# Image attention by GpSimd and by the output projection, idle products at the start, another order of exponentials

## The chip, the cores and the metric

The kernel runs on one core of a Trainium2 chip. The metric is the device time of one execution in microseconds, from start to end on that core.

## What is computed

Two cross-attention layers follow each other over a batch of 8, each on x of 256 rows by 320 channels, 20 heads of 16. The second has an image part with four image tokens; its weights are a softmax over the sum of scaled scores and a semantic term. Cut to what matters:

```python
# layer 0: text tokens 0..76, image tokens 77..255 of the context, two softmaxes
q, k, v = heads(x @ Wq.T), heads(text @ Wk.T), heads(text @ Wv.T)
out = softmax(q k^T / 4) v + softmax(q k_ip^T / 4) v_ip
x = out @ Wo.T + bo + x
# layer 1: text tokens 0..251, four image tokens
probs_t = softmax(q k^T / 4)
qsem = l2norm(probs_t @ text)                    # per head, 512 channels
sem = qsem @ l2norm(ip).T                        # per head, 4 tokens
probs_ip = softmax(q k_ip^T / 4 + 0.5 * sem) * mask[s]
out = probs_t v + probs_ip v_ip
x = out @ W_out + b_out + x
```

## The kernel before

A unit u is one batch element of one layer: units 0 to 7 are layer 0, 8 to 15 layer 1. A unit has ten steps (NP), one for each pair of heads; q = 10u + j counts steps. `plan(u, j)` (L96) writes out by hand the order of the work of a step, and every engine's program walks through the same plan and issues what is its own, in that order. A stretch u = -1 of ten steps stands ahead of unit 0. All waits are on counting semaphores.

What a step has, as TensorE sees it:

- `scores(q+1)` (L468, products at L476): two chunks of 512 columns for the next pair of heads. ScalarE makes exponentials of them into P (`weights`, L795). In layer 1 it first makes rounded ones into PH (`rounded_weights`, L786), chunk 0 and 1, and then the plain ones, chunk 0 and 1.
- in layer 1, GpSimd subtracts PH from P (Y, L1221), TensorE multiplies PH by the context's Gram matrix (`quad`, L480, products at L490), and VectorE multiplies both (Y, L1002); this gives the norm of qsem.
- `weigh` (L494) in every even step: values, the Gram part and the sums of four heads into the bank pPV (L508 and L512, in layer 1 L517 and L522; L522 waits for VectorE's Y of the last head pair). ScalarE takes it out (`evacuate`, L805, into Vs), `values_back` (L526, L531) transposes it, VectorE's `normalize` (L1004) divides and stores O and ST. GpSimd's `norms` (L1228) takes the power -0.5.
- `maximum(u+1, h)` (L447, L453): the row maxima of the next unit's scores, reduced by VectorE (L984, L985, L987, L989) into m_sb; how many fall into a step is in MAXH and, for u = -1, MAXF. `shift_rows` (L464) transposes them; rows go by DMA into the operand QP (L695, the high ones on ScalarE's queue in layer 0, the low ones on SyncE's), and `scores` of that unit wait for them.
- pieces of `prepare(u+2)` (L392, L374): the projections of the unit after next, so many products in each step as PACE says, and FIRST for u = -1. A job that ends has "done" in the plan; SyncE then stores its result (`store_queries`, `store_keys`) and later loads it as head rows (`load_queries`, `load_keys`, L671 and L679); the maxima wait for these.

The image part of a unit u of layer 1 is done in unit u+1: `image_softmax` (L1035, with the sum, the exponential by ScalarE at L827) in step 1, `image_shares` (L1054, w4 at L1068) in step 2, then one product per image token, w4 by the value row VB (`image_product`, L706, into one of two tiles TI that lie in VX), by GpSimd, and one addition to O for each by VectorE (`image_add`, L1081), in steps 3 to 5. For unit 14 VectorE does the products as well; the last unit is cut into heads 0 to 11 and 12 to 19, part of the first being done inside the unit. Then `attention_back` (L535, L545) transposes O in step 6, ScalarE and VectorE split it into ahi and alo (L714, L906), and `output` (L550, L560) multiplies by wo in steps 7 and 8, VectorE adds the residual (L1104), SyncE stores. At the very end `last_output` (L564, L572) runs in two parts, each behind its transposes. In layer 0 the same is in steps 1, 2, 4 and 5 of the next unit. `image_tokens` (L576, L583 to L595) makes the image keys, values and norms once, in step 3 of unit 1.

TensorE takes banks from a pool of seven, the one given back longest ago, and waits then until its last reader is done (`freed`, `take`). A DMA and a wait of SyncE hold up all that stands behind them on its queue. The values VB of the next image part are loaded on SyncE in step 5 (L1331).

## Time and profile before

| what | value |
|---|---|
| runs, us | 840.23, 841.76, 843.2 (median 841.76) |
| the profiled execution, us | 841.76 |
| its span, first to last instruction, us | 840.0 |
| mean granted clock of TensorE | 0.965 of 2.4 GHz |
| busy, share of the span | TensorE 92%, VectorE 71%, ScalarE 50%, GpSimd 45% |
| DMA | 101.94 MB, mean 121 GB/s |

Names of engines in the rows: PE is TensorE's products, PEld its weight loads, DVE VectorE, ACT ScalarE, POOL GpSimd, SPq and ACTq the queues that issue DMAs. A line such as L453 is one of the code. "x2" are two instructions that follow each other, and the time is from the start of the first to the end of the last; products overlap, since their drain is counted in. In brackets stands how long the engine stood idle before, and what ended it. The granted clock is given as a share of 2.4 GHz: 0.5 is the lower level, 1.2 GHz.

### The profile page before, as it was taken

The numbers are of one execution on the slowest core, as the hardware profiler recorded it, in microseconds if no ns is written. First come the engines' busy times: TensorE is split into PE (matmuls) and PEld (weight loads), VectorE is DVE, ScalarE is ACT, GpSimd is POOL, SyncE is SP. The second block draws the span as 40 slices with busy tenths as digits, with TensorE's granted clock in tenths as the row PEclk, the third lists the DMA queues.
The fourth block names the chain that finished last, engine by engine and source line by source line (L and its number), as shares of the span: only waits on it lengthen the run. The fifth ranks groups of instructions, "written<-read, shape, count | busy, mean of one in ns | idle before, by whom it ended". The sixth has DMA issues, their size and how long they took to land.

```text
span 840.0 us, 17139 instructions
## 1 busy us (share of the span) xinstructions
PE 773.8 (92%) x6304; PEld 626.1 (75%) x6304; DVE 594.3 (71%) x1571; ACT 424.1 (50%) x907; POOL 379.6 (45%) x283
## 2 busy tenths in 40 slices
PE   5679899999999999999999999999999999887774
PEld 5678688888888877877877777878777777654452
DVE  4357355757577576858679689698796895976784
ACT  5234535464636565565455564654655645444420
POOL 6421112020202031225587577676865776758561
PEclk9799999999999999999999999999999999999795
DMA  8865734665637463744263173351541533110010
GB/s 257 224 181 150 185 107 120 200 161 152 171 101 217 118 197 90 205 106 139 67 159 114 47 183 98 78 169 52 134 131 44 142 98 80 30 47 20 30 34 16
DMA packets 103171, 101.94 MB, mean 121 GB/s; under 512 B 10152, under 2 KB 102064, under 8 KB 103088
## 3 DMA queue, kind: packets, MB, share of 16 engines
q1 hardware_dynamic: 101552, 99.54, 42.7%
q10 hardware_dynamic: 1536, 1.31, 0.5%
q8 instruction: 50, 0.82, 0.4%
q14 instruction: 33, 0.27, 0.1%
HBM read 62.93 MB, written 36.74 MB: 119 GB/s over the span
## 4 chain that ended last, share of the span: by engine, by line
PE 68%; DVE 16%; issue 6%; DMA 4%; ACT 3%; POOL 1%; SPq 1%; ACTq 0%; DVEq 0%; POOLq 0%
PE pB L374 20%; PE pB L490 11%; PE pB L453 7%; PE pB L476 7%; PE pB L560 5%; DVE m_sb L987 4%; PE pPV L512 4%; PE pPV L522 4%; PE pPV L517 3%; PE pB L531 3%; PE pPV L508 2%; DVE Y L1002 2%; DVE O L1081 2%; DMA KP<-k0d 1%; PE pB L545 1%
## 5 line engine op out<-in xcount | busy, mean ns | idle before, releaser
L1221 POOL TENSOR_TENSOR Y<-P,wv 128x512 f32<-128x512 f32 x120 | 157.2, 1325 | 146.2 <-ACT P L803 146.1
L1002 DVE TENSOR_TENSOR Y<-pB,Y 128x512 f32<-128x512 f32 x160 | 107.9, 683 | 58.1 <-PE pB L490 49.9
L453 PE MATMUL pB<-KP,QP 96*128 96x256 f32 x640 | 131.0, 289 | 11.9 <-DMA KP<-k0d 10.3
L453 PEld LDWEIGHTS pB<-KP,QP 96*128 96x128 f32 x640 | 108.3, 193 | 24.8 <-DMA KP<-k0d 6.8
L476 PE MATMUL pB<-QP,KP 100*128 100x512 f32 x320 | 111.8, 427 | 9.8 <-DMA QP<-mhi 4.5
L987 DVE TENSOR_REDUCE m_sb<-pB 128x2 f32<-128x504 f32 x160 | 107.6, 674 | 9.6 <-PE pB L453 8.7
L1198 POOL TENSOR_TENSOR klo<-xin,khi 128x256 fp32r<-128x256 f32 x18 | 13.2, 756 | 217.2 <-ACT khi L714 217.2
L803 ACT ACTIVATE P<-pB 128x512 f32<-128x512 f32 x160 | 86.5, 596 | 43.5 <-PE pB L476 33.7
L803 ACT ACTIVATE P<-pB,ln 128x512 f32<-128x512 f32 x160 | 101.3, 693 | 0.0
L793 ACT ACTIVATE wv<-pB 128x512 fp32r<-128x512 f32 x120 | 66.9, 592 | 65.1 <-PE pB L476 64.8
L714 ACT ACTIVATE Vs<-pPV 128x512 f32<-128x512 f32 (+1 forms) x80 | 39.4, 493 | 118.9 <-PE pPV L512 72.5
L984 DVE TENSOR_REDUCE m_sb<-pB 128x2 f32<-128x154 f32 x160 | 49.8, 311 | 49.3 <-PE pB L453 48.8
L985 DVE TENSOR_REDUCE m_sb<-pB 128x2 f32<-128x358 f32 x160 | 83.2, 520 | 0.0
L490 PE MATMUL pB<-wv,wk 128*128 128x512 f32 x250 | 77.9, 416 | 0.1
L374 PE MATMUL pB<-chi,wki 128*128 128x180 f32 (+3 forms) x384 | 71.3, 274 | 0.0
L374 PE MATMUL pB<-khi,wq 128*128 128x256 f32 (+1 forms) x288 | 58.5, 300 | 8.4 <-DVE wq L906 8.4
L476 PEld LDWEIGHTS pB<-QP,KP 100*128 100x128 f32 x320 | 51.4, 193 | 16.5 <-DVE Y L1002 5.8
L1228 POOL TENSOR_TENSOR rn<-n,mhalf 128x8 f32<-128x8 f32 (+2 forms) x17 | 57.8, 3397 | 12.2 <-DVE n L1033 12.1
L374 PE MATMUL pB<-wvi,chi 128*128 128x320 f32 x256 | 62.1, 312 | 0.2 <-POOL wvi L1211 0.2
L374 PEld LDWEIGHTS pB<-chi,wki 128*128 128x128 f32 (+1 forms) x384 | 56.1, 172 | 6.0 <-issue 4.1
L490 PEld LDWEIGHTS pB<-wv,wk 128*128 128x128 f32 x250 | 45.2, 194 | 18.6 <-issue 10.7
L522 PE MATMUL pPV<-Y,y 128*32 128x256 f32 x640 | 44.5, 398 | 12.4 <-DVE Y L1002 12.4
(159 smaller groups left out, 1698.2 us busy)
## 6 DMA issues: line engine op xcount, KB each, us to landing
QP<-q0d SPq DMA_DIRECT2D x64, 192.0 KB, 4.0
KP<-k0d SPq DMA_DIRECT2D x64, 192.0 KB, 4.2
c_sb<-in_cT SPq DMA_DIRECT2D x16, 512.0 KB, 4.9
q0d<-qhi SPq DMA_DIRECT2D x32, 256.0 KB, 2.5
k0d<-khi SPq DMA_DIRECT2D x30, 256.0 KB, 2.5
VB<-vipd SPq DMA_DIRECT2D x8, 640.0 KB, 3.6
q0d<-qlo SPq DMA_DIRECT2D x16, 256.0 KB, 2.7
k0d<-klo SPq DMA_DIRECT2D x15, 256.0 KB, 2.6
```

The lines of the kernel that those rows point to most:

```text
L374: made = mm(out, l, r, start=(n == 0), stop=(n == len(pairs) - 1))
L453: made = mm(bank[:, sc * S:sc * S + S], QP[i][0:KROWS, j, a, sc * 128:sc * 128 + 128], KP[i][0:KROWS, j, :], start=True, stop=True)
L476: mm(bank[:, :], KP[i][0:QROWS, j, ch * 128:ch * 128 + 128], QP[i][0:QROWS, j, :, :].rearrange("p a s -> p (a s)"), start=True, stop=True) ...
L490: made = mm(bank[:, :], G[i][:, col:col + 128], ph[src], start=(n == 0), stop=(n == len(jobs) - 1))
L522: made = mm(pPV[32 * j:32 * j + 32, 0:S], y21[:, :], Y[:, p, ch, ss], start=False, stop=(ch == 1), tile_position=(0, 32 * j))
L793: act(PH[q % HR][ch], bank_of["sc", q, ch][:, :], ACT.Exp, scale=0.25).then_inc(ac_ph, 1)
L803: act(P[:, q % PR, ch, :], bank_of["sc", q, ch][:, :], ACT.Exp, scale=0.25, **twice).then_inc(ac_exp, 1)
L985: nc.vector.tensor_reduce(m_sb[:, :, H + h], v[:, :, TXT0:S], AX, ALU.max).then_inc(dv_mx, 1)
L987: nc.vector.tensor_reduce(m_sb[:, :, h], v[:, :, 0:TXT1], AX, ALU.max)
L1002: tt(Y[:, p, dst, :], bank_of["gp", q, dst][:, :], Y[:, p, dst, :], MUL).then_inc(dv_y, 1)
L1221: tt(Y[:, p, ch, :], P[:, p, ch, :], PH[q % HR][ch].bitcast(F32), SUB).then_inc(po_y, 1)
L1228: tt(rn[:, :, hs], n2[:, :, hs], mhalf[:, 0:2 * n].rearrange("p (c h) -> p c h", c=2), POW).then_inc(po_rn, 1)
```

## The change

What it does, part by part:

1. **Start.** After `prepare(0)` TensorE issues thirty products of 512 columns whose result nobody reads (`repeat`). FIRST is 9 products in each of the steps 0 to 8 of u = -1 and 30 in step 9 (before 12 in eight steps, 8 and 7). In steps (0, 0) and (1, 0) the first maximum stands behind the weigh part and two of the three pieces, no longer ahead of them.
2. **Exponentials.** ScalarE's order in layer 1 is rounded 0, plain 0, rounded 1, plain 1; in even steps the evacuation stands behind rounded 0.
3. **Image part of units 8 to 13** ("folded"): GpSimd makes four products and the three additions of them in TI (`image_step`, one step of seven at the end of step 2, two at the end of steps 3, 4 and 5); VectorE adds once, in step 6. The transposes are in step 7, the output in 8 and 9. VB is loaded in step 7. w4 has a tile of its own.
4. **Image part of units 14 and 15** ("closing"): the image values of the heads are laid out as block-diagonal tiles bdh and bdl (`image_values`, VectorE, six products with a mask hmask that a new DMA loads, and two memsets once), multiplied by wo to Mb (nine products of TensorE, taken out by ScalarE); w4 is transposed (two, `image_weights_back`, wT by ScalarE); Mb and wT are one more product, in f32, in each chunk of the output. O of these units holds the text part alone. For unit 14 this is in steps 2 to 6 of unit 15; for unit 15 bd and Mb are in steps 7 and 8, and all else behind the last values: transposes of O, the 24 products of the output, the image softmax, shares, transposes, copy and three products.
5. **image_tokens** also makes the values transposed (twelve more products), split into vhi and vlo. cip, csq, vhi, vlo and the mask share a tile.

The diff, cut:

```diff
-FIRST = (12, 12, 12, 12, 12, 12, 12, 12, 8, 7)
+FIRST = (9, 9, 9, 9, 9, 9, 9, 9, 9, 30)
+LATE_MAX = ((0, 0), (1, 0))
...
+    elif (u, j) in LATE_MAX:
+        out += scores + weigh
+        rest = heads
...
+    if u > B and folded(u - 1):
         if j == 1:
-            out += [("soft", u - 1, 0)]
+            out += [("soft", u - 1)]
         if j == 2:
-            out += [("shares", u - 1, 0), ("mix", u - 1, 0, 0)]
+            out += [("shares", u - 1)]
+        out += [("mix", u - 1, n) for n in {2: (0,), 3: (1, 2), 4: (3, 4), 5: (5, 6)}.get(j, ())]
+        if j == 6:
+            out += [("add", u - 1)]
+        if j == 7:
+            out += [("ot", u - 1, 0), ("ot", u - 1, 1)]
+        if j in (8, 9):
+            out += [("op", u - 1, (8, 9).index(j))]
+    elif u > B:
+        if j == 1:
+            out += [("soft", u - 1)]
+        if j == 2:
+            out += [("shares", u - 1), ("ot", u - 1, 0)]
         if j == 3:
-            out += [("mix", u - 1, 0, 1), ("mix", u - 1, 0, 2), ("add", u - 1, 0, 0)]
+            out += [("ot", u - 1, 1), ("wt", u - 1), ("bd", u - 1)]
         if j == 4:
-            out += [("mix", u - 1, 0, 3), ("add", u - 1, 0, 1), ("add", u - 1, 0, 2)]
-        if j == 5:
-            out += [("add", u - 1, 0, 3)]
-        if j == 6:
-            out += [("ot", u - 1, 0), ("ot", u - 1, 1)]
-        if j in (7, 8):
-            out += [("op", u - 1, j - 7)]
+            out += [("mb", u - 1)]
+        if j in (5, 6):
+            out += [("op", u - 1, j - 5)]
...
+    if (u, j) == (U - 1, 7):
+        out += [("bd", u)]
+    if (u, j) == (U - 1, 8):
+        out += [("mb", u)]
...
+                if u == U - 2:
+                    pe.wait_ge(ac_wt, closing_no(u))
+                    pe.wait_ge(ac_mb, closing_no(u))
...
+                    if u == U - 2:
+                        made = mm(bank[0:M, n * S:n * S + S], Mb[:, m * 128:m * 128 + M], wT[:, :], start=False, stop=True)
...
+            def last_image(u):
+                pe.wait_ge(ac_wt, closing_no(u))
+                pe.wait_ge(ac_mb, closing_no(u))
+                for m in range(KC):
+                    mm(bank_of["op", u, m][0:CHUNK[m], 0:S], Mb[:, m * 128:m * 128 + CHUNK[m]], wT[:, :],
+                       start=False, stop=True).then_inc(pe_op, 1)
...
+                bank = take("idle", n)
+                for _ in range(n):
+                    mm(bank[:, :], wki[:, 0, 0, 0:128], wki[:, 0, 1:3, 0:256], start=True, stop=True)
+                give(bank)
...
             for _ in prepare(0):
                 pass
+            repeat(30)
...
                 for ch in range(2):
+                    if ch and q >= B * NP:
+                        rounded_weights(q, ch)
...
+                for v, dst in ((vhi, bdh), (vlo, bdl)):
+                    for k in range(KC):
+                        K = CHUNK[k]
+                        made = tt(dst[0:K, k], v[0:K, k, None, NIP * b:NIP * b + NIP].bitcast(F32).to_broadcast([K, H, NIP]),
+                                  hmask[0:K, k, :, None].to_broadcast([K, H, NIP]), MUL)
+                made.then_inc(dv_bd, 1)
...
+                if n in (0, 1, 3, 5):
+                    tt(heads(TI[:, at]), w4[:, :, :, token:token + 1].to_broadcast([128, 2, H, D]),
+                       heads(VB[:, token, None, :].to_broadcast([128, 2, C])), MUL).then_inc(po_q, 1)
+                else:
+                    tt(TI[:, 0], TI[:, 0], TI[:, 1], ADD).then_inc(po_mix if n == 6 else po_q, 1)
...
-                    if u >= B and j == 5:
+                    if folded(u) and j == 7:
                         load_image_values(u)
```

## Rows read from the trace of the kernel before

**Rows 1.** Busy time by stretch: us, engines' busy time, granted clock, DMA, GB/s.

```profile
32.70:59.10 26.40, 21.84 (x154) 21.53 (x154) 17.14 (x49) 6.43 (x18) 2.09 (x3) 0.88 0.69 190
...
93.40:142.00 48.60, 44.82 (x387) 36.83 (x385) 25.14 (x76) 20.77 (x49) 9.63 (x7) 0.96 0.49 136
142.00:179.70 37.70, 37.62 (x347) 31.79 (x344) 24.67 (x74) 20.24 (x46) 4.26 (x6) 1.00 0.66 181
...
537.60:593.50 55.90, 55.15 (x443) 44.35 (x442) 46.32 (x117) 31.27 (x66) 38.27 (x26) 1.00 0.40 111
...
705.30:758.20 52.90, 46.22 (x341) 33.09 (x340) 40.82 (x100) 25.85 (x50) 37.76 (x26) 0.94 0.22 57
758.20:805.00 46.80, 37.03 (x242) 24.82 (x241) 33.24 (x59) 22.35 (x43) 32.13 (x20) 0.85 0.07 23
805.00:840.00 35.00, 18.31 (x122) 11.79 (x120) 22.16 (x53) 4.25 (x11) 12.62 (x11) 0.71 0.09 28
```

**Rows 2.** Timeline, TensorE, before unit 0: start, us, engine line, shapes, [idle before].

```profile
32.72 0.80 PE L453 MATMUL pB<-KP,QP 96*128 96x256 f32 x2 [6.56 <-DMA KP<-k0d]
...
59.10 1.85 PE L476 MATMUL pB<-QP,KP 100*128 100x512 f32 x4 [4.54 <-DMA QP<-mhi]
```

**Rows 3.** Timeline, TensorE, from the start of unit 1.

```profile
99.22 0.47 PE L453 MATMUL pB<-KP,QP 96*128 96x256 f32 x2 [3.78 <-DMA KP<-k0d]
...
100.08 1.68 PE L512 MATMUL pPV<-P,VY 128*32 128x256 f32 x16
...
109.91 1.05 PE L512 MATMUL pPV<-P,VY 128*32 128x256 f32 x16
...
116.37 2.45 PE L583 MATMUL pB<-cip,Y 128*128 128x32 f32 x24
118.75 2.34 PE L589 MATMUL pB<-Y,cip 128*32 128x320 f32 x8
```

**Rows 4.** Timeline, GpSimd, steps 2 to 6 of unit 11.

```profile
560.61 1.34 POOL L706 TENSOR_TENSOR VX<-tw,VB 128x640 f32<-128x640 f32 x1 [0.74 <-DVE tw L1068]
...
578.30 1.30 POOL L1221 TENSOR_TENSOR Y<-P,wv 128x512 f32<-128x512 f32 x1 [2.42 <-ACT P L803]
```

**Rows 5.** Groups by shape, GpSimd: the full two-input pass of 640 elements.

```profile
L1208 POOL TENSOR_TENSOR wo<-c_sb,wo 128x640 fp32r<-128x640 f32 x1 | 1.6, 1553 | 3.0 <-ACT wo L714 3.0
```

**Rows 6.** Instructions on the tile VX (TI): minimum, median and maximum in ns.

```profile
L1081 DVE TENSOR_TENSOR O<-O,VX x36: 424/817/2030, 452.7 to 830.1; 128x640 f32<-128x640 f32 x28, 128x384 f32<-128x384 f32 x4, 128x256 f32<-128x256 f32 x4
L706 POOL TENSOR_TENSOR VX<-tw,VB x28: 643/1337/1925, 448.9 to 829.0; 128x640 f32<-128x640 f32 x24, 128x384 f32<-128x384 f32 x2, 128x256 f32<-128x256 f32 x2
```

**Rows 7.** Timeline, unit 14, steps 4 to 6.

```profile
737.08 3.13 DVE L1081 TENSOR_TENSOR O<-O,VX 128x640 f32<-128x640 f32 x2
...
742.13 1.93 PE L522 MATMUL pPV<-Y,y 128*32 128x256 f32 x16 [2.92 <-DVE Y L1002]
```

**Rows 8.** Timeline, unit 15, steps 4 to 6.

```profile
784.48 1.89 PE L490 MATMUL pB<-wv,wk 128*128 128x512 f32 x7
...
794.63 1.93 PE L522 MATMUL pPV<-Y,y 128*32 128x256 f32 x16 [4.51 <-DVE Y L1002]
```

**Rows 9.** Timeline, the end of unit 15 and of the kernel.

```profile
805.78 0.25 DVE L1043 TENSOR_TENSOR t<-ST,invip 128x96 f32<-128x96 f32 x1
...
806.06 1.22 DVE L1046 TENSOR_TENSOR t<-t,rn 128x96 f32<-128x96 f32 x1
...
817.74 1.93 PE L522 MATMUL pPV<-Y,y 128*32 128x256 f32 x16 [3.03 <-DVE Y L1002]
...
820.90 0.21 DVE L1015 RECIPROCAL rs<-pB 128x8 f32<-128x8 f32 x1 [2.16 <-PE pB L531]
...
822.03 1.89 POOL L1228 TENSOR_TENSOR rn<-n,mhalf 128x8 f32<-128x8 f32 x1 [2.34 <-DVE n L1033]
...
834.01 1.05 PE L572 MATMUL pB<-ahi,wo 128*128 128x256 f32 x4
...
837.02 0.47 DVE L1113 SCALAR_TENSOR_TENSOR xres<-pB,bo,xres 64x256 f32<-64x256 f32 x1 [0.58 <-PE pB L572]
```

More of the change, by code:

```diff
@@ L63, in norms_no, with folded, closing_no @@
     return 2 * (u - B) + list(norm_parts(u)).index(g) + 1
[L66 to L89 removed]
+def folded(u):
+    return B <= u < U - 2
+def closing_no(u):
+    return u - (U - 2) + 1
 def thirds(n):
@@ L344, in freed @@
                     pe.wait_ge(dv_y, 2 * (a - B * NP) + what[2] + 1)
+                elif kind == "idle":
+                    pass
                 elif kind == "nt":
@@ new lines, in image_values @@
+            def image_values(u):
+                bank = take("mb", u)
+                pe.wait_ge(dv_bd, closing_no(u))
+                pe.wait_ge(lo_w["o1"], 1)
+                pairs = []
+                for k in range(KC):
+                    h_, l_ = (v[:, k].rearrange("p h n -> p (h n)") for v in (bdh, bdl))
+                    pairs += [(h_, wo[:, 0, k, :]), (h_, wo[:, 1, k, :]), (l_, wo[:, 0, k, :])]
+                for _ in chain(bank[0:H * NIP, 0:C], pairs, pe_mb):
+                    pass
+                give(bank)
@@ new lines, in image_tokens @@
+            def image_tokens():
+                for i, w in enumerate((wki1, wvi1)):
+                    bank = take("ip", i)
+                    pe.wait_ge(l_w["ip1"], 32)
+                    pe.wait_ge(l_w["const"], 16 * 6)
+                    for m in range(KC):
+                        M = CHUNK[m]
+                        for k in range(EC):
+                            made = mm(bank[0:M, 32 * m:32 * m + 32], w[:, k, m * 128:m * 128 + M], cip[:, k, :],
+                                      start=(k == 0), stop=(k == EC - 1))
+                    made.then_inc(pe_ip, 1)
+                    give(bank)
@@ L597, in image_tokens, with repeat @@
                 give(bank)
+                bank = take("ip", 3)
+                for k in range(EC):
+                    made = mm(bank[0:B * NIP, 0:C], cip[:, k, :], wvi1[:, k, :], start=(k == 0), stop=(k == EC - 1))
+                made.then_inc(pe_ip, 1)
+                give(bank)
+            def repeat(n):
+                bank = take("idle", n)
+                for _ in range(n):
+                    mm(bank[:, :], wki[:, 0, 0, 0:128], wki[:, 0, 1:3, 0:256], start=True, stop=True)
+                give(bank)
             for _ in prepare(0):
                 pass
+            repeat(30)
             for u in range(-1, U):
@@ L633, in tensor_program @@
                 attention_back(U - 1, part)
[L634 removed]
+            last_output(U - 1)
+            image_weights_back(U - 1)
+            last_image(U - 1)
         def two(bank, M, n):
@@ L891, in scalar_program @@
             evacuate(U - 1, NG - 1)
-            image_weights(U - 1, 1)
-            attention_back(U - 1, 0)
-            attention_back(U - 1, 1)
+            for part in range(2):
+                attention_back(U - 1, part)
+            image_weights(U - 1)
+            image_weights_back(U - 1)
         def low_c(u):
```

326 lines of the change are left out of this document (159 added, 167 removed).

## The prediction

> **What bounds the kernel now.** I read the windows by unit first. The page has no single limit: in layer 1 TensorE is full, at both ends it is not. Unit 11 stands for units 10 to 13: TensorE is busy 55.15 of 55.90 us, VectorE 46.32, GpSimd 38.27, so nothing done beside TensorE there is worth more than 0.75 us [rows 1]. The start is different: in the stretch before the first scores TensorE is busy 21.84 of 26.40 us at clock 0.88, and unit 1 takes 48.60 us where unit 2 takes 37.70 [rows 1]. The end is worst: in unit 14 TensorE is busy 46.22 of 52.90 us, then 37.03 of 46.80 at clock 0.85, then 18.31 of 35.00 at 0.71 [rows 1]. So each part of the change is priced in its own stretch. The profiled execution took 841.76 us, which is also the median of the three runs; the span is 840.0, so 1.76 lies around it and the sum is made from 841.76.
>
> **Start: idle products, FIRST, LATE_MAX.** TensorE stands 6.56 us until the first head rows land, and its first products then run at the 1.2 GHz level (two products of 256 columns in 0.80 us) [rows 2]. Thirty products of 512 columns at the 2.4 GHz level need about 7 us (seven quads of that size start within 1.89 less one's drain, 0.235 each [rows 8]), so they fill the hole and end about when the rows land; they can overrun by 0.5 us. What they buy is 3 us of TensorE time behind the hole. But the way to the first scores is VectorE's: 20 maxima and the splits, 17.14 us busy in 26.40 [rows 1], and it starts waiting only where TensorE is slow. With FIRST at nine products a step the last maximum is issued after 72 products, not 96. Twenty-four products at half rate's 0.21 or full rate's 0.12 us are 3 to 5 us, of which I count 3, VectorE being the next limit: the last maximum some 3 us earlier. Against this, the job KT now ends in step 8, so on SyncE's queue the five to six key stores (about 3 us of issue) stand ahead of the low rows of the shifts; the high rows, on ScalarE's queue, are not behind them. The first scores start at about 56.6, not 59.10 [rows 2]: **-2.5** for the first scores (bounds -3.8 and +0.5, if the stores push the low rows past the old time). The 30 products left for step 9 cover most of the wait of 4.54 us [rows 2].
>
> Step 0 of unit 1: TensorE waits 3.78 us for unit 2's rows and comes back at 1.2 GHz, where the sixteen products of its second part take 1.68 us, and 1.05 later [rows 3]. With LATE_MAX the weigh (2.0 us at speed) and eight products (1.2 us) go ahead of that wait; they have their data. The landing itself doesn't move against the unit. **-4.0** (bounds -5 and -2). For (0, 0) the same order costs nothing and keeps TensorE busy while unit 1's keys, which are now stored later, land.
>
> image_tokens gets a third group of twelve products, like the first, which took 2.45 us for 24 instructions [rows 3], plus small copies: **+2.5** (+2.3 to +3.5, as ScalarE now waits for the end of all of them). The load of the head mask and the split of the values are once and small. Start in all: -4.0.
>
> **Units 9 to 13.** GpSimd's part of a unit goes from four products to four products and three additions. A product of 640 elements took 1.34 us [rows 4]; the nearest full two-operand pass of 640 elements took 1.553 [rows 5]. So 4 x 1.34 + 3 x 1.55 = 10.0 us against 5.4: +4.6 us of GpSimd a unit. In the trace the room for it is there: from the first product at 560.61 until it has waited 2.42 us for ScalarE at 578.30 [rows 4] are 17.7 us, in which GpSimd has six roundings of about 1.29 and four products (13.1), and for the rest stands still or is stretched, mostly by VectorE's additions. After the change the same window holds 7.7 + 10.0 = 17.7. Laid out by the plan (one image step at the end of step 2, two at the ends of 3, 4 and 5), the last addition ends at about 578.2, before the next rounding has its data. VectorE loses three of four additions (median 0.82 us, up to 2.03 beside GpSimd [rows 6]), which now and then delay its product with the rounding, and so TensorE. One addition in step 6 remains, and the transposes behind it move from step 6 to 7, the output from 7 and 8 to 8 and 9. The result's stores and, queued behind them on SyncE, the loads of the next keys wait for VectorE's residual; the output's place is later, but TensorE gets there earlier by what was moved (16 products, about 1.9 us), so I price that at nothing; if it is wrong the first maximum of the next unit waits up to 1.6 us. **-0.4 each, -2.0** for five units (bounds: the 0.75 of idle, -3.7, and +1.6 each, +8).
>
> **ScalarE's order.** Rounded, plain, rounded, plain: GpSimd can start one exponential earlier (0.55 us), the second rounded chunk is ready one later. Its user is TensorE's quad in the next step, which comes 1.5 us or more after; in even steps the evacuation stands ahead of both. In a full unit: nothing. If that cover is gone it costs 0.6 us a step at most.
>
> **Unit 14 (image of 13).** Two additions in a row, 3.13 us [rows 7], delay the product with the rounding; TensorE waits 2.92 us and comes back at 1.2 GHz (1.93 us for sixteen products instead of 1.05) [rows 3, 7]. That goes: -4.4 with the quads after it. But here a step takes 4 to 5 us, and GpSimd needs 2 x 1.29 + 1.34 + 1.55 = 5.5 in each of three: it falls 2 to 3 us behind, and the transposes in step 7 wait for the addition. **-2.7** (-4.4 to +1).
>
> **Unit 15.** Four products and four additions of VectorE for image 14 go; they held the weigh of step 6 for 4.51 us, which then ran at half rate [rows 8]. In their place: two transposes, nine products for Mb (1.35 us) and one f32 product for each output chunk. An f32 product of 320 columns is two instructions, eight took 2.34 us [rows 3], so 256 columns cost about 0.45 and three 1.3 us. The output (now steps 5 and 6, before 7 and 8) fills what was idle, so up to step 6 little is won. Behind it: the softmax of the first twelve heads delayed ScalarE's exponentials, and TensorE waited some 2 us for that; then the shares and one addition delayed the last weigh to 817.74 with 3.03 us idle, at half rate [rows 9]. Without them the last weigh starts after the quads and GpSimd's last rounding: I lay it out at about 810.9. **-7** (-10 to -2). The new work there is bd: six small two-input products for each of the last two images. The nearest row is 0.25 us for 96 elements free and 1.22 for the same size beside GpSimd's rounding [rows 9]; two held and four free, 3.4 us, is what I take, about as much as the softmax steps that leave.
>
> SBUF — State Buffer in the Trainium skill (section Who interferes with whom) says that a VectorE instruction with two SBUF inputs contends with a GpSimd instruction that reads SBUF, and that the loser blocks fully. The 1.22 against 0.25 agrees. By that rule this change has GpSimd busy longer and would hold such instructions oftener; that is the third rival.
>
> **The end.** From the first instruction on the last transposed values (820.90) to the last residual (837.02 + 0.47) are 16.6 us [rows 9]: softmax of eight heads, two products by each engine, four additions, transposes, splits, 15 products. After: values, norms and power 3.1 (the power took 1.89 [rows 9]); five softmax steps of about 0.35 for 160 elements, 1.7; exponential 0.4; shares 1.3; two transposes 0.4; copy 0.45; three f32 products 1.3; residual 0.5: 9.2 us at the 2.4 GHz level. The transposes, splits and 24 products of the text part run beside it. At 1.2 GHz the 24 products take 5.1 (four in 1.05 less overlap [rows 9]) and push the closing behind them, and the f32 products double: 13. The trace has the lower level there; fewer holes speak for the higher. I take the middle, 11.1: **-5.5** (-7.4 to -3.6).
>
> **Sum.** -4.0 - 2.0 - 2.7 - 7 - 5.5 = -21.2: 841.76 - 21.2 = 820.6 us.
>
> **Rivals.** (1) *The ends give half*: VectorE, not TensorE, paces the maxima so that the first scores come where they were (+2.5), GpSimd falls behind in unit 14 (+2.7), the low clock stays at the end (+2) and unit 15 gives only 3 (+4): 832. For it: VectorE is busy 17.14 of those 26.40 us, and both ends of the stretch are waits for data [rows 1, 2]. Against: the trace has its waits just where TensorE is slow, at the start. (2) *GpSimd becomes the bound in layer 1*: the side other than mine. Its window is full, and 3 us is about what lies between a rounding and its use, so it decides once the seven image steps take over 0.4 us longer each than priced. At 1.93 each, the longest product seen [rows 6], they take 13.5 and it is 3.5 us late; passed on in units 9 to 14 with the loads of keys late as well (4 a unit, 24) it gives 820.6 + 24 + 2 = 846.6. Against: the waits of today that vanish. (3) *The builds are held*: each of the six small products waits for a whole GpSimd instruction, 6 x 1.3 = 7.8 us instead of 3.4, twice, and the softmax in the closing units too: +8, 829. That is what the page's rule gives in its strict form; the trace so far shows such instructions held while GpSimd has a queue and free in between, so I give it less. (4) *It doesn't do what it says*: the idle products or the late maxima fill nothing since the data come later by as much: +5, 826.
>
> **How the numbers follow.** Forecast 0.55, rival 1 0.18, rival 2 0.06, rival 3 0.13, rival 4 0.08. The forecast's own range from the bounds is 812 to 829; rivals 3 and 4 lie in it or at its edge, rival 1 needs 832. Low 811, high 832. A measurement of this kernel can tell about 0.3%, 2.5 us. Faster by more: all but rival 2 and a small rest, 0.91; within it 0.04; slower 0.05.
>
> **What would show it.** Start: first scores at 56 to 57 us instead of 59.1, granted clock near 1 from 33 us; no wait of 3.8 us in step 0 of unit 1, that unit at some 47 us. Units 10 to 13 at 55.2 to 55.7; GpSimd 43 us busy in each, VectorE 43. If GpSimd's roundings wait for nothing over whole units and TensorE waits for VectorE's product, rival 2 is true. Unit 14: no wait of the weigh, but one of the transposes in step 7. Unit 15: the last weigh some 7 us nearer to the unit's start, bd instructions between 0.2 and 1.3 us. The end: 9 to 13 us from the last values. The prediction is wrong if SyncE's queue holds head rows longer than now, or if GpSimd's additions cost well over 1.6 us.

## The result, and the profile after

The changed kernel takes 821.82 us (median of 4 runs, 820.88 to 822.45) where the kernel before took 841.0 beside it (839.1 to 843.2): a ratio of 0.977, with the interval 0.9743 to 0.9797. The forecast was 820.6. The profiled execution took 820.88 us with a span of 819.1 and a mean granted clock of 0.985 (before: 0.965).

Busy time by stretch in the kernel after, the stretches that answer to [rows 1] (columns: from:to and length in us; busy time and count on PE, PEld, DVE, ACT, POOL; granted clock, DMA share, GB/s):

```profile
32.70:56.40 23.70, 19.37 (x155) 18.79 (x154) 16.53 (x49) 5.51 (x16) 1.07 (x3) 1.00 0.81 205
...
89.90:143.10 53.20, 50.91 (x411) 41.21 (x409) 25.26 (x78) 21.01 (x51) 9.66 (x7) 0.90 0.46 125
...
370.40:426.50 56.10, 54.61 (x431) 43.23 (x429) 41.99 (x103) 31.84 (x69) 29.45 (x21) 1.00 0.44 119
...
538.00:593.10 55.10, 55.00 (x442) 44.26 (x441) 44.11 (x113) 31.26 (x66) 42.90 (x30) 1.00 0.40 113
703.30:752.50 49.20, 44.24 (x340) 32.39 (x339) 38.61 (x98) 25.83 (x50) 42.06 (x29) 0.97 0.19 48
752.50:790.00 37.50, 33.51 (x252) 23.84 (x251) 22.92 (x51) 20.12 (x41) 25.28 (x17) 0.95 0.08 26
790.00:819.00 29.00, 22.44 (x154) 16.06 (x152) 15.77 (x44) 7.85 (x17) 14.67 (x9) 0.88 0.09 25
```

These are the way to the first scores, unit 1, unit 8, unit 11, unit 14 and unit 15 in two pieces. TensorE's idle time in unit 11 has gone from 0.75 us to 0.10 (55.00 busy of 55.10). Two units have become longer: unit 1, with 53.2 us at clock 0.90, and unit 8, with 56.1 us.

A unit starts with its first scores product. Between these starts the two traces differ as follows:

| stretch | before | after | measured | forecast |
|---|---|---|---|---|
| up to the first scores | 59.10 | 56.39 | -2.7 | -2.5 |
| unit 0 | 34.30 | 33.53 | -0.8 | 0 |
| unit 1, first wait (late maxima) | 10.39 | 7.36 | -3.0 | -4.0 |
| unit 1, step with the image tokens | 8.16 | 15.13 | +7.0 | +2.5 |
| unit 1, the rest | 30.04 | 30.65 | +0.6 | 0 |
| units 2 to 7 | 227.3 | 227.4 | +0.1 | 0 |
| unit 8 | 54.43 | 56.05 | +1.6 | 0 |
| units 9 to 13 | 281.6 | 276.8 | -4.8 | -2.0 |
| unit 14 | 52.89 | 49.20 | -3.7 | -2.7 |
| unit 15 to the second part of the last weigh | 59.56 | 50.74 | -8.8 | -7 |
| from there to the last values | 3.16 | 2.05 | -1.1 | (0) |
| last values to last residual | 16.6 | 11.3 | -5.3 | -5.5 |

The rows add up to -20.9 us, the forecast to -21.2. That the total is so close is luck: two costs that were sized too low (6.1 us together: tokens, unit 8) met gains in layer 1 and at the end that were sized too low as well. The rows of the start come from one trace each, and there equal instructions differ from trace to trace: in nine kernels that are the same up to unit 1 the first scores come between 55.2 and 57.2 us, and unit 0 takes 33.2 to 35.7 us.

Timeline of TensorE after, from the idle products to unit 1 (start, us, engine line, shapes, in brackets the idle time before and what ended it). The lines up to 56.39 answer to [rows 2], those behind to [rows 3]:

```profile
25.82 6.99 PE L640 MATMUL pB<-wki 128*128 128x512 f32 x30
34.19 0.47 PE L458 MATMUL pB<-KP,QP 96*128 96x256 f32 x2 [1.38 <-DMA KP<-k0d]
...
49.84 0.38 PE L469 MATMUL pB<-ident,m_sb 128*40 128x128 f32 x2 [1.16 <-DVE m_sb L1040]
56.39 0.96 PE L481 MATMUL pB<-QP,KP 100*128 100x512 f32 x3 [1.78 <-DMA QP<-mlo]
...
96.84 0.47 PE L458 MATMUL pB<-KP,QP 96*128 96x256 f32 x2 [2.29 <-DMA KP<-k0d]
...
110.07 6.35 PE L620 MATMUL pB<-cs,Y 128*128 128x32 f32 x48
116.36 1.92 PE L627 MATMUL pB<-cs,ones 128*128 128x32 f32 x8
118.20 4.48 PE L632 MATMUL pB<-Y,cs 128*32 128x320 f32 x8
122.61 1.11 PE L481 MATMUL pB<-QP,KP 100*128 100x512 f32 x2
```

The thirty idle products cost 6.99 us of time that was idle, and the products behind them start at the upper level: two of 256 columns in 0.47 us, 0.80 in the kernel before. The wait before the first scores is for the low rows, which stand behind the key stores on SyncE's queue, as the prediction had it. In unit 1 the eight value products take 4.48 us where they took 2.34: TensorE has fallen to 1.2 GHz in the middle of the block, without having stood still once.

### The profile page after: what moved, and what is told of

The parts are those of the page before. It is cut to its first block, busy times and chain, and to the rows that moved or that the text cites. A ratio compares the mean times of both kernels' runs of the same rounds, so it can differ in the third digit from the quotient of the medians.

```text
span 819.1 us, 17251 instructions
## 1 busy us (share of the span) xinstructions
PE 781.8 (95%) x6392; PEld 633.5 (77%) x6392; DVE 564.1 (69%) x1539; ACT 424.9 (52%) x911; POOL 402.7 (49%) x297
## 4 chain that ended last, share of the span: by engine, by line
PE 75%; DVE 9%; DMA 4%; issue 4%; POOL 3%; ACT 3%; SPq 2%; POOLq 0%; DVEq 0%; ACTq 0%
PE pB L379 21%; PE pB L495 13%; PE pB L458 8%; PE pB L481 7%; PE pB L579 5%; PE pPV L522 4%; PE pPV L517 4%; PE pPV L527 4%; PE pB L536 3%; PE pPV L513 2%; DMA KP<-k0d 2%; DVE m_sb L1042 2%; POOL Y L1281 2%; DVE m_sb L1040 1%; ACT P L843 1%
## 5 line engine op out<-in xcount | busy, mean ns | idle before, releaser
L458 PEld LDWEIGHTS pB<-KP,QP 96*128 96x128 f32 x640 | 106.3, 191 | 20.7 <-issue 10.2
L481 PE MATMUL pB<-QP,KP 100*128 100x512 f32 x320 | 108.9, 420 | 3.6 <-DMA QP<-mlo 1.8
L843 ACT ACTIVATE P<-pB,ln 128x512 f32<-128x512 f32 x160 | 110.6, 691 | 0.0
L831 ACT ACTIVATE wv<-pB 128x512 fp32r<-128x512 f32 x120 | 71.2, 593 | 51.2 <-PE pB L481 50.4
L1304 POOL TENSOR_TENSOR rn<-n,mhalf 128x8 f32<-128x8 f32 (+2 forms) x17 | 57.1, 3358 | 15.8 <-DVE n L1088 15.8
L379 PE MATMUL pB<-khi,wq 128*128 128x256 f32 (+1 forms) x288 | 56.4, 292 | 8.3 <-DVE wq L961 8.3
L481 PEld LDWEIGHTS pB<-QP,KP 100*128 100x128 f32 x320 | 50.2, 191 | 8.2 <-DMA QP<-mlo 2.4
L379 PEld LDWEIGHTS pB<-khi,wq 128*128 128x128 f32 (+1 forms) x288 | 43.5, 179 | 12.0 <-DVE wq L961 8.3
```

The source lines that it names most:

```text
L379: made = mm(out, l, r, start=(n == 0), stop=(n == len(pairs) - 1))
L458: made = mm(bank[:, sc * S:sc * S + S], QP[i][0:KROWS, j, a, sc * 128:sc * 128 + 128], KP[i][0:KROWS, j, :], start=True, stop=True)
L481: mm(bank[:, :], KP[i][0:QROWS, j, ch * 128:ch * 128 + 128], QP[i][0:QROWS, j, :, :].rearrange("p a s -> p (a s)"), start=True, stop=True) ...
L831: act(PH[q % HR][ch], bank_of["sc", q, ch][:, :], ACT.Exp, scale=0.25).then_inc(ac_ph, 1)
L843: act(P[:, q % PR, ch, :], bank_of["sc", q, ch][:, :], ACT.Exp, scale=0.25, **twice).then_inc(ac_exp, 1)
L1304: tt(rn[:, :, hs], n2[:, :, hs], mhalf[:, 0:2 * n].rearrange("p (c h) -> p c h", c=2), POW).then_inc(po_rn, 1)
```

## Experiments

The kernels ran on other chips than the first comparison, each beside the kernel before; where medians of different groups are compared, the ratios are used.

**The image tokens, in four steps.** The same products, but one group in each of steps 3, 4, 5 and 7 of unit 1:

```diff
-    if (u, j) == (1, 3):
-        out += [("ip",)]
+    if u == 1 and j in (3, 4, 5, 7):
+        out += [("ip", (3, 4, 5, 7).index(j))]
...
```

> The changed kernel (821.8 us), with its image-token products no longer in one block in step 3 of unit 1 but in four groups at the ends of steps 3, 4, 5 and 7, projections between them. The changed kernel took 12.75 us for the block (48 products instructions of 32 columns 6.35, ones 1.92, values 4.48), at the 1.2 GHz level from its middle on. Theory A, that a long run of narrow products lowers TensorE's clock: in four groups all run at the upper level, 2.45 + 2.34 + 1.08 + 2.45 = 8.3 us, so 4.4 us go, and the granted clock of unit 1 goes from 0.90 to near 1; about 817.4. Theory B, that the block waits for something (banks, ScalarE's copies, VectorE) and the clock falls for that: the same waits come at the four places and at most 1 us goes; about 821.

Measured 818.2 us, ratio 0.9712 (0.9659 to 0.9765). TensorE's timeline of this kernel:

```profile
110.23 2.45 PE L621 MATMUL pB<-cs,Y 128*128 128x32 f32 x24
...
114.40 1.93 PE L517 MATMUL pPV<-P,VY 128*32 128x256 f32 x16
...
120.76 2.34 PE L626 MATMUL pB<-Y,cs 128*32 128x320 f32 x8
...
133.88 2.45 PE L621 MATMUL pB<-cs,Y 128*128 128x32 f32 x24
...
137.45 1.95 PE L517 MATMUL pPV<-P,VY 128*32 128x256 f32 x16
```

Every token group now has the price of the upper level. But the weigh right behind each group of 24 runs at the lower one (sixteen products in 1.93 and 1.95 us, 1.05 at speed), and unit 1 took 52.8 us against 53.1 (its granted clock is 0.90 in both): in the profile the split moved the loss more than it removed it. The steps from the first token group to the end of the unit took 34.1 us against 35.6, and the first two intervals 0.8 us more. The time agrees with theory A's 817.4, the clock of this profile does not.

**The image tokens with wide products among them.** Two products of 512 columns with no use behind every eight narrow ones:

```diff
+                        if m < KC - 1:
+                            repeat(2)
                     made.then_inc(pe_ip, 1)
                     give(bank)
+                    repeat(2)
```

> The changed kernel with the image-token block left in one piece, but with two idle products of 512 columns after every chunk of four narrow ones (twelve idle products in all, 2.8 us at the upper level). They only add work. Theory A (narrow products lower the clock, wide ones hold it): the block takes 8.3 + 2.8 = 11.1 us instead of 12.75, and stays at the upper level: 1.6 us less than the changed kernel, about 820. Theory B (waits, or a clock that falls for another reason): 12.75 + 2.8 to 5.6, so 3 to 5 us more, about 826.

Measured 821.03 us, ratio 0.9748 (0.9703 to 0.9794). The clock holds through the whole block, and the values take 2.34 us again:

```profile
112.01 0.98 PE L620 MATMUL pB<-cs,Y 128*128 128x32 f32 x8
112.82 0.71 PE L643 MATMUL pB<-wki 128*128 128x512 f32 x2
...
120.83 2.34 PE L635 MATMUL pB<-Y,cs 128*32 128x320 f32 x8
```

The block lasts 11.1 us instead of 12.5, as theory A says, and the timeline has no idle time of TensorE in it in either kernel. So narrow products are what brings the clock down. In the time the wide ones hardly pay: twelve of them cost 2.8 us, and the step with the block takes 13.7 us, where it takes 13.9 to 15.1 in five kernels with the block as changed and the same instructions ahead of it.

**ScalarE's order as before.** In layer 1 both rounded exponentials stand again ahead of both plain ones:

```diff
-                    if ch and q >= B * NP:
-                        rounded_weights(q, ch)
...
                             rounded_weights(*a, 0)
+                            rounded_weights(*a, 1)
```

> The changed kernel with ScalarE's old order of exponentials (rounded 0, rounded 1, plain 0, plain 1), all else as in it. I had priced the order at nothing. But unit 8 takes 1.6 us longer in the changed kernel than before, and there GpSimd starts one exponential earlier beside VectorE's splits of the context, two of which took 1.40 and 2.18 instead of 0.42 and 1.09 us. Theory A (the new order makes GpSimd and VectorE meet in unit 8): unit 8 back to 54.4, and nothing else in the full units, while units 14 and 15, where GpSimd's start counts, lose up to 1.5: 820 to 822. Theory B (unit 8 lost for another reason, the order is worth its half microsecond a step wherever the step is not full): unit 8 stays at 56.0 and the kernel is 1 to 3 us slower.

Measured 821.08 us, ratio 0.9749. Unit 8 is back at 54.42 us (56.05), units 10 to 13 stay at 55.1 to 55.2 and unit 9 at 56.45: theory A. The time doesn't show the 1.6 us; in this profile units 0 and 1 took 3.2 us longer than in the changed kernel's, with the same instructions. What happens in unit 8 is seen in VectorE's and GpSimd's timelines. Changed kernel:

```profile
373.08 2.86 POOL L1281 TENSOR_TENSOR Y<-P,wv 128x512 f32<-128x512 f32 x2 [30.20 <-ACT P L843]
373.40 1.40 DVE L961 TENSOR_TENSOR khi<-xin,khi 64x256 fp32r<-64x256 f32 x1
376.56 2.18 DVE L961 TENSOR_TENSOR clo<-c_sb,chi 128x256 fp32r<-128x256 f32 x3
379.40 0.49 PE L481 MATMUL pB<-QP,KP 100*128 100x512 f32 x1 [0.60 <-DVE Y L1057]
```

With the old order:

```profile
376.37 0.42 DVE L960 TENSOR_TENSOR khi<-xin,khi 64x256 fp32r<-64x256 f32 x1
376.54 2.66 POOL L1280 TENSOR_TENSOR Y<-P,wv 128x512 f32<-128x512 f32 x2 [30.87 <-ACT P L841]
378.24 1.25 DVE L960 TENSOR_TENSOR clo<-c_sb,chi 128x256 fp32r<-128x256 f32 x1
```

GpSimd's first roundings of layer 1 start 3.14 us after unit 8's first scores with the old order and 2.65 us after with the new one (units 8 start at 373.40 and 370.43). VectorE's split of the last rows begins 2.97 us after the first scores in both: started ahead of GpSimd it takes 0.42 us, behind it 1.40, and the next splits follow late. SBUF — State Buffer in the Trainium skill (section Who interferes with whom) has just this pair, a VectorE instruction with two SBUF inputs and a GpSimd one. The trace agrees: the VectorE instruction is held, and GpSimd's two roundings take 2.86 and 2.66 us, where they take 2.53 alone. Of the 1.6 us of unit 8, 1.1 are idle time of TensorE (1.5 us against 0.4); the longest of these waits, 0.60 us, is for VectorE's late product.

**Idle products in the holes of the end.** Fourteen products of 512 columns in five waits behind the last weigh:

```diff
             weigh(U - 1, NG - 1)
+            repeat(2)
             values_back(U - 1, NG - 1)
+            repeat(2)
             for part in range(2):
                 attention_back(U - 1, part)
+            repeat(6)
             last_output(U - 1)
+            repeat(2)
             image_weights_back(U - 1)
+            repeat(2)
             last_image(U - 1)
```

> The changed kernel with idle products of 512 columns put into TensorE's holes behind the last weigh: 2, 2, 6, 2 and 2 of them, 3.3 us at the upper level, placed where it waits for ScalarE or VectorE. In the changed kernel 11.3 us pass from the first instruction on the last values to the end, with the 24 products and the three f32 ones at the 1.2 GHz level. Theory A (the level falls for the short holes of 0.5 to 1.5 us): the 24 products take 2.9 instead of 5.1 us and the f32 ones 0.9 instead of 1.7; the image weights are then the last to come, at about 6.9 us, so the end is at 9.3, 2 us less. Theory B (the level falls anyway, or the idle products run at the lower one themselves and are in the way): 0 to 2 us more.

Measured 819.56 us, ratio 0.9731. In the changed kernel TensorE is at the lower level in the last output, here at the upper:

```profile
810.01 1.05 PE L591 MATMUL pB<-ahi,wo 128*128 128x256 f32 x4
```

```profile
808.05 0.64 PE L591 MATMUL pB<-ahi,wo 128*128 128x256 f32 x4
...
811.72 1.71 PE L597 MATMUL pB<-VX 80*128 80x256 f32 x6
```

The first line is the changed kernel's, the other two are this one's. From the start of the last weigh's second part to the end of the span the changed kernel takes 15.8 us and this one 14.3. The three f32 products of the image (L597, six instructions) take 1.71 us in both kernels; the granted clock is 1.00 there in both (from 813 us on in the changed kernel, 0.51 in the five us before), so 1.71 is their price at speed, and theory A's 0.9 for them is wrong. Seven other kernels without these idle products took 15.0 to 15.8 us there, but the one with ScalarE's old order took 14.3 too, and all four with them took 14.3: the level at the end varies, and in every trace with the idle products it was the upper one for the 24 products.

**Without the idle products at the start.**

```diff
-            repeat(30)
```

> The changed kernel without its thirty idle products ahead of the first maxima; all else as changed. Theory A (idle products bring the clock, FIRST brings the order, VectorE is the next limit): TensorE stands some 7 us before its first products, these run at the lower level (256 columns in about 0.4 us each instead of 0.12), the shift transposes' wait of 1.16 us for VectorE and the wait of 1.78 us for the low rows take up most of the 3 us lost: first scores at 57 to 58 us instead of 56.39, the time 1 to 2 us longer than the changed kernel's. Theory B (the idle products alone brought the 2.7 us): first scores at 59.1, the time 2.7 us longer. Theory C (they bring nothing, the landings set it): first scores within 0.3 us of 56.4.

Measured 818.08 us, ratio 0.9722 (0.9685 to 0.976): no slower than the changed kernel, and its interval meets that one's. TensorE in this kernel:

```profile
33.32 0.80 PE L458 MATMUL pB<-KP,QP 96*128 96x256 f32 x2 [6.72 <-DMA KP<-k0d]
...
57.05 1.21 PE L481 MATMUL pB<-QP,KP 100*128 100x512 f32 x3 [1.73 <-DMA QP<-mlo]
...
109.96 4.94 PE L620 MATMUL pB<-cs,Y 128*128 128x32 f32 x48
...
115.97 3.83 PE L632 MATMUL pB<-Y,cs 128*32 128x320 f32 x8
```

From the landing of the first head rows to the first scores are 23.7 us, 22.2 in the changed kernel's trace. Nine traces with its instructions up to there take 22.0 to 24.2 us, three without the idle products 23.7 to 24.4: about 1 us in the mean. So the first scores fit theory A (57.05), but lie within what equal kernels show. On the time theories A and B are both wrong. The second interval of unit 1, which holds the wait for unit 2's rows, ends at 98.6 us here and at 98.7 in the changed kernel: SyncE issues these rows 1.2 us later (89.67 us against 88.43), but from the issue to the end of the wait are 7.1 us instead of 8.4. So it is in all three kernels without the idle products (7.0 to 7.1), and nine with them and both late maxima have 8.0 to 8.5; why, no run shows. And the same 48 token products take 4.94 us instead of 6.35, the clock falling later in the block. Nothing of the block differs between the two kernels, but that can't be put down to the edit: of four other kernels with the changed one's instructions up to the block, three take 5.40 to 5.49 us for them and one 6.29.

**Unit 1 without the late maxima.**

```diff
-LATE_MAX = ((0, 0), (1, 0))
+LATE_MAX = ((0, 0),)
```

> The changed kernel with the late maxima in step 0 of unit 0 only; step 0 of unit 1 has its maxima ahead of the weigh again. Theory A: TensorE waits some 3.8 us there for unit 2's rows and comes back at the lower level; the first interval of unit 1 goes from 7.4 back to about 10.4 us and the time rises by 3 us. Theory B (the landing moves with the unit, or later waits of unit 1 take the loss up, TensorE having idle time in step 1 too): the sum of the first two intervals of unit 1 changes by under 1 us, the time by 0 to 1 us.

Measured 822.88 us, ratio 0.9786 (0.9738 to 0.9833). The first two intervals of unit 1 go from 8.8 to 12.7 us: a wait of 3.39 us and a return at the lower level, as theory A says. The time shows about 1 of these 3.9 us, less than these intervals can tell; in the profile the part of unit 1 behind these two intervals was shorter here (42.6 us instead of 44.4), for the most part in the step with the tokens (13.7 instead of 15.1).

**All four additions by VectorE.** GpSimd makes the four products only:

```diff
-        out += [("mix", u - 1, n) for n in {2: (0,), 3: (1, 2), 4: (3, 4), 5: (5, 6)}.get(j, ())]
-        if j == 6:
-            out += [("add", u - 1)]
+        out += [("mix", u - 1, n) for n in {2: (0,), 3: (1, 2), 4: (3,)}.get(j, ())]
+        out += [("add", u - 1, n) for n in {3: (0,), 4: (1, 2), 5: (3,)}.get(j, ())]
...
```

> The changed kernel with GpSimd making the four products of an image only; VectorE makes all four additions (steps 3, 4, 4 and 5), in units 9 to 14; transposes and output stay where the change has put them. Theory A (the gain in layer 1 is VectorE's three additions gone): units 9 to 13 go from 55.10 back to 55.7 to 55.9 us each, unit 14 from 49.2 to 51 or more, the time 4 to 7 us longer; GpSimd 38.3 us busy a unit, VectorE 46.3. Theory B (the gain is the later place of transposes and output, which lets no wait stand in TensorE's queue): units 9 to 13 stay at 55.1 to 55.3 and the time within 1.5 us.

Measured 827.73 us, ratio 0.9827 (0.9781 to 0.9874). Theory A is right: units 10 to 13 take 55.90 to 55.97 us, and unit 14 takes 52.4. The windows of units 11 and 14, and two lines of the timeline:

```profile
537.50:593.40 55.90, 55.02 (x442) 44.39 (x441) 47.59 (x117) 31.18 (x67) 38.79 (x27) 1.00 0.39 111
708.00:760.40 52.40, 45.35 (x339) 33.31 (x339) 41.99 (x101) 25.77 (x51) 37.20 (x27) 0.93 0.16 45
```

```profile
566.62 2.01 DVE L1126 TENSOR_TENSOR O<-O,VX 128x640 f32<-128x640 f32 x1
...
576.34 0.50 PE L480 MATMUL pB<-QP,KP 100*128 100x512 f32 x1 [0.71 <-DVE Y L1056]
```

An addition beside GpSimd takes 2.01 us, VectorE's product with the rounding comes late, and TensorE waits 0.71 us for it once a unit. That is nearly the whole difference in unit 11 (55.90 us against 55.10). The later place of transposes and output gives nothing of its own.

**More work for GpSimd.** One more product of 640 elements in each of steps 3, 4 and 5:

```diff
-                po.wait_ge(po_q, 6 * k + n)
+                extra = 1 if n in (1, 3, 5) else 0
+                at_q = (6 + 3 * 1) * k + n + 1 * (n // 2)
+                for e in range(extra):
+                    po.wait_ge(po_q, at_q + e)
+                    tt(heads(TI[:, at]), w4[:, :, :, token:token + 1].to_broadcast([128, 2, H, D]),
+                       heads(VB[:, token, None, :].to_broadcast([128, 2, C])), MUL).then_inc(po_q, 1)
+                po.wait_ge(po_q, at_q + extra)
```

> The changed kernel with one more product of 640 elements on GpSimd in each of steps 3, 4 and 5 of units 9 to 14, its result thrown away: about 4.0 us more of GpSimd a unit (46.9 busy of 55.1). Theory A (the prediction's second rival with its threshold: some 3 us lie between a rounding and its use, so what is above that is passed on to TensorE): units 9 to 13 lengthen by 1 to 3 us each, unit 14 by 3 to 4 (there GpSimd has no room at all), the time by 8 to 18 us. Theory B (GpSimd's 12 us of idle time a unit can be used in any step, since a late rounding only moves its queue): units 9 to 13 lengthen by under 0.3 us each, the time by under 4 us, all of it in unit 14.

Measured 832.57 us, ratio 0.9879 (0.9837 to 0.9921). Units 10 to 13 take 56.05 to 56.10 us instead of 55.10, unit 14 54.8 instead of 49.2. Theory A holds, at the low end of its range in units 9 to 13 (1.0 us each) and above it in unit 14 (5.6 us). GpSimd, VectorE and TensorE in unit 11 of this kernel:

```profile
566.10 1.34 POOL L1300 TENSOR_TENSOR VX<-w,VB 128x640 f32<-128x640 f32 x1 [1.66 <-DVE w L1119]
...
588.03 1.89 DVE L1125 TENSOR_TENSOR O<-O,VX 128x640 f32<-128x640 f32 x1 [2.00 <-POOL VX L1303]
...
590.36 0.63 PE L549 MATMUL pB<-ident,O 128*128 128x128 f32 x4 [1.39 <-DVE mlo L961]
...
594.64 1.30 POOL L1281 TENSOR_TENSOR Y<-P,wv 128x512 f32<-128x512 f32 x1 [1.08 <-ACT P L843]
```

From 566.10 on GpSimd waits for nothing until 594.64, VectorE's addition waits 2.00 us for GpSimd's last one, and TensorE's transposes 1.39 for VectorE. Of 4.0 us added, 1.0 is passed on: the changed kernel has about 3 us of room in GpSimd's row of steps, though GpSimd stands still for 12.2 us of every unit (42.90 busy of 55.10).

**FIRST as before.**

```diff
-FIRST = (9, 9, 9, 9, 9, 9, 9, 9, 9, 30)
+FIRST = (12, 12, 12, 12, 12, 12, 12, 12, 8, 7)
```

> The changed kernel with the old FIRST (12 products a step beside the maxima, then 8 and 7); idle and late maxima as changed. Theory A (as the prediction had it: nine a step bring the last maximum some 3 us forward): first scores at about 58.5 to 59 us instead of 56.4. Theory B (TensorE being at the upper level from the first product, VectorE's maxima pace that stretch and the order is worth at most 1 us): first scores at 56 to 57.3. On the time, both: since unit 2's rows land at 98 to 99 us in every run whatever the first scores did, at most 1.5 us of either shows; 821 to 824.

Measured 821.12 us, ratio 0.9723 (0.9697 to 0.9749). The first scores come at 56.57 us, behind a wait of 4.79 for the low rows. Theory B: with the idle products in, the order of the products is worth nothing that can be seen among the 55.2 to 57.2 us of equal kernels.

**Parts together.** Three kernels with ScalarE's old order (both rounded exponentials first, as in the kernel before) and the idle products at the end:

> The changed kernel with three parts together: image tokens in four groups in four steps, both exponentials of a text unit in the old order in layer 1's ScalarE (plain, rounded for chunk pairs as before the change), and wide idle products in the five waits of the end. Theory A (the gains are apart in place, so they add: order -1.6, end -1.8, tokens -0.3 to -3.6 as measured alone): 815 to 817 us. Theory B (tokens and end were worth less than a run of theirs showed, noise of the landings): 818 to 820.

> As the kernel with all parts, but the image tokens in one block, as changed, and without the thirty idle products at the start. Theory A (the idle products buy nothing that lasts, the place where the clock falls in the token block is what moved the kernel without them): 815 to 818 us, with the block's four groups of twelve at 1.2, 1.1, 1.4 and 1.0 to 1.7 us. Theory B (idle products are worth the 0.7 to 1.5 us of first scores): over 818.

> As the kernel with all parts, without the thirty idle products at the start. Against the kernel with all parts it prices the idle products once more: Theory A (the wait for unit 2's rows takes up what the first scores lose): the same within 1 us, unit 1's first waits shorter by what the start is late. Theory B: 1 to 2.5 us longer.

| kernel | median, us | runs | ratio | first scores | unit 1 |
|---|---|---|---|---|---|
| tokens split, idle products at the start | 815.78 | 813.75 to 818.91 | 0.9671 (0.9647 to 0.9696) | 55.87 | 49.4 |
| tokens whole, none at the start | 816.32 | 813.89 to 819.25 | 0.9675 (0.9648 to 0.9701) | 55.58 | 50.2 |
| tokens split, none at the start | 813.75 | 811.06 to 817.0 | 0.9645 (0.9619 to 0.9671) | 56.83 | 50.3 |

All three beat the changed kernel, whose interval begins at 0.9743, above theirs. The gains of order and end are there in each (unit 8 takes 54.4 to 54.5 us, the way from the last weigh's second part to the end 14.3), and the time lies where theory A has it. The idle products at the start buy nothing that the time shows; the third kernel is the fastest seen, though its interval meets the others'. In the first of the three, the weigh behind the tokens ran at the upper level, with the same products in the same order as in the first split kernel, where it did not:

```profile
114.81 1.05 PE L517 MATMUL pPV<-P,VY 128*32 128x256 f32 x16
```

## Why the prediction was right, and where it was not

**Start, first scores: right.** -2.7 against -2.5, with the wait for the low rows named. The prediction gave the 3 us to FIRST and the clock together, and neither is needed beside the other: with the old FIRST the first scores come at 56.57 us, without the idle products at 55.6 to 57.1, with both at 55.2 to 57.2, against 59.10 in the kernel before, with neither. Most of it lasts. SyncE issues unit 2's rows 3.5 us earlier than before (columns: start, length of the issue; kernel before, then changed kernel):

```profile
91.90 1.43 SPq L679 DMA_DIRECT2D KP<-k0d  x2
```

```profile
88.43 1.45 SPq L730 DMA_DIRECT2D KP<-k0d  x2
```

TensorE's wait for them ends at 96.84 us instead of 99.22, and with the late maxima out the second interval of unit 1 still ends at 102.68 instead of 105.21. So rival 4's mechanism ("the data come later by as much") is false of the start as a whole; it is seen in small for the idle products alone, whose microsecond the wait for these rows takes up.

**Late maxima: -3.0 against -4.0.** The mechanism was right: the clock stays at 1.00 and eight products and the weigh go ahead of the wait. The step that failed is "The landing itself doesn't move against the unit": from unit 1's first scores to the end of the wait are 5.8 us before and 6.9 after, so that 2.29 us of the wait stay (0.9 in the kernels without idle products, where it is 5.5 to 5.6). Undone alone, it costs 3.9 us in these intervals.

**Image tokens: the term that was mis-sized, +7.0 against +2.5.** The third group was priced at the first one's 2.45 us for 24 [rows 3]. That price holds only while the clock does. Now 64 narrow products stand in a row (48 for keys and values, 8 for the norms, 8 with 32 columns of weights) where 40 stood, and the clock drops in the middle. The prediction took a row at the upper level and assumed the level; both token experiments show the dearer part to be the clock's, not the products': of the 7.0 us about 2.4 are the third group and 4.6 the lower level. With the same instructions this step took 13.9 us in three other kernels and 15.1 in one, so +5.8 to +7.0 is what the change costs there. The Trainium skill (TensorE: Matmul & The Clock Gate, Part 1: The HAM clock gate) says that the clock is set by how busy the engine has been of late. The trace agrees only in part: TensorE is busy 8.00 of 8.00 us from 115 to 123 us, and the granted clock is 0.50 all the while, so the busy time that the profile counts did not decide it.

**ScalarE's order: 0 against +1.6.** The fault is in "in a full unit: nothing": unit 8, the first with GpSimd's roundings, is not full, and there an earlier GpSimd meets VectorE's splits. The prediction asked who uses the rounded chunk, and not what GpSimd's earlier start would collide with.

**Units 9 to 13: -4.8 against -2.0.** About 0.95 of it is the output part that now stands behind the start of the next unit and comes back in unit 15. The rest is 0.76 a unit, the whole of TensorE's idle time, the lower bound of the text's own range (-3.7). The caution was GpSimd's full window; GpSimd was busy 42.90 us, the 43 of the text, and has about 3 us of room left. This is rival 2's threshold: the 3 us that the prediction named as lying between a rounding and its use, measured with 4.0 us of added work. Rival 2 needed 3.5 us of lateness and did not get it, since the image steps cost what was priced:

```profile
L1294 POOL TENSOR_TENSOR VX<-w,VB x24: 1327/1338/1357, 451.7 to 740.5; 128x640 f32<-128x640 f32 x24
L1297 POOL TENSOR_TENSOR VX<-VX x18: 1552/1572/1583, 456.9 to 741.9; 128x640 f32<-128x640 f32 x18
L1125 DVE TENSOR_TENSOR O<-O,VX x6: 814/814/1907, 472.2 to 743.5; 128x640 f32<-128x640 f32 x6
```

(Instructions on the tile VX in the kernel after: count, then minimum, median and maximum in ns; answering to [rows 6].)

**Unit 14: -3.7 against -2.7.** The transposes do wait for the addition, but 0.63 us instead of the 2 to 3 expected.

**Unit 15 and the end: -15.2 against -12.5.** The last weigh's second part waits 0.55 us (3.03 in [rows 9]). The six small products are not held: 1 us for six, each time, where 3.4 had been put in. That is the term that was mis-sized, and rival 3 did not come. GpSimd stands still beside the first six and runs its power (792.60 to 796.76 us) beside the second; so it is in twelve of the thirteen kernels (in the other one product meets the last 0.17 us of a rounding and takes 0.27 us), and what whole roundings beside them would have cost no run shows. The trace before had the hint: there a VectorE product of 96 elements beside the power took 0.26 us (at 815.04), one beside a rounding 1.22 [rows 9].

```profile
776.57 0.99 DVE L1180 TENSOR_TENSOR VB<-cs 128x80 fp32r<-128x80 f32 x6
...
795.06 0.98 DVE L1180 TENSOR_TENSOR VB<-cs 128x80 fp32r<-128x80 f32 x6
...
803.25 1.07 PE L527 MATMUL pPV<-Y,y 128*32 128x256 f32 x16 [0.55 <-DVE Y L1057]
...
805.30 0.21 DVE L1070 RECIPROCAL rs<-pB 128x8 f32<-128x8 f32 x1 [2.10 <-PE pB L536]
...
815.23 1.40 DVE L1153 SCALAR_TENSOR_TENSOR xres<-pB,bo,xres 128x256 f32<-128x256 f32 x3 [3.02 <-PE pB L597]
```

(VectorE and TensorE, timeline after.) The last two lines bound the end: 805.30 to 816.63, 11.3 us for a forecast of 11.1, half way between the clocks; TensorE is at the lower level for the 24 products, and the six f32 instructions are dearer than priced (1.71 against 1.3). The 24 products took 4.9 us, and 3.1 in the kernel with idle products at the end.

What is not settled: why the clock falls earlier or later in the same block of narrow products. Up to the end of the block the kernels with ScalarE's old order and with more work for GpSimd have the changed kernel's instructions (6.35 us), and yet:

```profile
114.63 5.47 PE L620 MATMUL pB<-cs,Y 128*128 128x32 f32 x48
```

```profile
114.06 5.40 PE L620 MATMUL pB<-cs,Y 128*128 128x32 f32 x48
```

So it varies from one execution to the next, and a difference of 1 us in one profile of this block proves nothing about an edit.

## What to carry to other kernels

A gain ahead of a transfer's landing counts only if the transfer moves with it; ask of every early gain which landing stands behind it, and read the time of its issue in both traces. Where equal kernels differ by more than the gain, one pair of traces can't price it: compare the same stretch in every trace that has the same instructions there. A price read at one clock level is a price with a condition: when a change lengthens a run of narrow products, price it at both levels, and the work behind it too. Before moving an engine's start forward, look at what its neighbour does in just that stretch, above all in the first unit of a new phase, which is unlike the full ones; and to know how much room an engine has, add work to it rather than read its busy share (12 us idle a unit here, 3 us of room).

## What the runs showed of the hardware

TensorE fell from the 2.4 to the 1.2 GHz level without an idle gap, in a run of products of 32 columns (granted clock 1.00 up to 112 us, 0.50 from 114 to 122), and held with two products of 512 columns behind every eight narrow ones. In which part of the block it fell varied with equal instructions (48 products in 5.40 to 6.35 us). At the upper level six f32 instructions of 256 columns and 80 rows took 1.71 us, 0.29 apiece, as much as those of 320 columns [rows 3], where 1.3 had been worked out. VectorE's small two-input products (80 elements, 0.16 us apiece) were not held beside GpSimd's power, while a split of 256 elements beside its rounding took 1.40 instead of 0.42 us. In the trace before it was the same with products of one size, 96 elements: 0.26 us beside the power, 1.22 beside a rounding. It mattered what GpSimd was doing.
